# A second gate beside the attention steps: its calls spread anew over four steps, its softmax by tanh, another order within a step

## The chip, the core and the metric

The kernel runs on one core of one Trainium2 chip. The core has five engines with queues of their own: TensorE (PE in the profile; PEld is its weight load), VectorE (DVE), ScalarE (ACT), GpSimd (POOL) and SyncE (SP), which here only issues DMAs. The metric is the device time of one execution in microseconds.

## The reference

The input is x of 2 x 4096 tokens with 256 features. Three sublayers follow each other: half of a feed-forward network of experts, an attention of the delta-rule kind, and the same feed-forward network again with the same weights. All of it is in fp32.

```
x = x + 0.5 * ffn(layernorm(x))
x = x + attn(layernorm(x))
x = x + 0.5 * ffn(layernorm(x))

ffn:  scores = softmax(x @ gate_w)                  # 8 experts
      top_scores, top_idx = top_k(scores, 2)
      y = sum over the two of  (silu(xs@w1) * (xs@w3)) @ w2,   xs = score * x

attn: q, k, v = silu(causal conv of 4 taps (x @ Wq, Wk, Wv)),  4 heads of 64;  q, k normed
      beta = sigmoid(x @ Wb)
      chunks of 64 tokens, in order:  A = I + tril(Kb K^T, -1);  T = A^-1;  W = T Kb;  U = T Vb
      mid = U - W S^T;  O = Q S^T + (Q K^T * M) mid;  S += mid^T K
      out = rmsnorm(O) * rms_w @ Wo
```

## The kernel before, in words

Three programs follow each other: `ffn` (the first), `attention`, `ffn` (the second). A feed-forward part works on rows sorted by expert. So before it, a gate scores each token, picks its two experts and scatters the token's row into the lists of both. The first gate runs at the start of the first `ffn`. The second gate works on the result of the attention, and it is woven into `attention`: it is what this change is about.

`attention` goes over 32 steps. A step takes 128 tokens of each of the two sequences. It is a software pipeline of five depths: `body(f, g, t, s, u, v)` is called once per step for each engine, with `f` for the projections, convolution and silu of the newest tokens, `g` for the small matrices between keys, `t` for their inversion by blocks, `s` for the state, the output and its projection, `u` for what the gate needs of one step's result (a turn of it, its logits, its mean and variance), and `v = (n, c)` for the gate of block n, which is 4 steps (8 tiles of 128 tokens). c counts the four steps over which the calls of one block are spread. It goes 1, 2, 3 and then 0, and the texts below call these the phases: a step of phase 1 is one in which c is 1, and so on. `LAST` is 7, the last block. Each engine runs its calls strictly in the order in which `body` has them, and waits on semaphores for the others. There is no scheduler: the order is written by hand.

What the gate does, before the change:
- phase 1: GpSimd `gate_pow` (1/std), VectorE `gate_norm` (four small instructions) between `first_out32` and `out_scale`, and at the end of the step `gate_first` (the largest logit, five instructions).
- phase 2: VectorE `gate_second` (six) and `gate_sums` (three) behind the convolution; ScalarE `gate_exps`, an Exp, between `silus(f, 1)` and `silus(f, 2)`.
- phase 3: VectorE `gate_scores`, `gate_row_ends`, `gate_ends`, `gate_places`; TensorE `positions` (three fp32 products) ahead of `out_project`.
- The rows of a block are loaded by SP (`load_rows`, one 256 KB load in a step) and scattered by GpSimd (`gate_scatter`, one indirect DMA for each of the 8 tiles): three tiles in phase 0, two in phase 1, three in phase 2.

What bounds a step is a loop through the engines: `x_turn` (TensorE) turns the normed tokens, ScalarE and VectorE split them in a high and a low part (`x_high`, `x_low`), TensorE projects (`qkv`), ScalarE copies out (`raw_out`), VectorE does the convolution (18 instructions of `conv`, L1665), ScalarE the silus, TensorE turns keys and values back (`turn_back`, L1307 and L1313), ScalarE takes squares (L2090) and `norm_in` prepares the next tokens. Beside that, TensorE carries the chain of `t` and `s`: L1403 (`second_products32`, needs VectorE's `first_out32`, L1733), L1547 (`out_turn`, needs `out_scale`, L1770), L1415 and L1417 (`first_products64`, needs ScalarE's `second_out32`, L2136), L1556 (`out_project`), L1429 (`second_products64`), and of the gate L1448 (`gate_turn`) and L1462 (`gate_products`). `keep_busy` and `fill` (L1247) are products of the identity whose result nobody reads.

The inverses of the small blocks go through DRAM: SP stores them when GpSimd has solved them (`collect_inverses`, L1202), and loads them in another layout when that has landed (`place_inverses`, L1209). TensorE turns them in the next step (`turn16`, L1346).

## Time and profile before

| | us |
|---|---|
| median of three executions | 1480.89 |
| lowest, highest | 1477.67, 1484.17 |
| the profiled execution, its own time | 1484.35 |
| its span in the profile | 1482.7 |
| the 32 attention steps, first `x_turn` to last | 385.0 to 1124.8 |
| PE, DVE, ACT, POOL busy, of the span | 88%, 73%, 60%, 61% |

The shares are means over three programs with different limits. Between 475 and 1125 us, where all depths of the pipeline are filled, a step repeats every 22.9 to 26.4 us, and PE is busy in nearly all of it. Steps are told apart by the start of L1261, the first product of `x_turn`. A wait stands in square brackets behind the instruction that waited: `[1.82 <-ACT ws L2084]` means that the engine sat idle for 1.82 us, and what came last was ACT's line 2084. PE rows have their count in hardware instructions, two for one fp32 product.

### The profile page before, as it was taken

The numbers are of one execution on the slowest core, as the hardware profiler recorded it, in microseconds if no ns is written. First come the engines' busy times: TensorE is split into PE (matmuls) and PEld (weight loads), VectorE is DVE, ScalarE is ACT, GpSimd is POOL, SyncE is SP. The second block draws the span as 40 slices with busy tenths as digits, with TensorE's granted clock in tenths as the row PEclk, the third lists the DMA queues.
The fourth block names the chain that finished last, engine by engine and source line by source line (L and its number), as shares of the span: only waits on it lengthen the run. The fifth ranks groups of instructions, "written<-read, shape, count | busy, mean of one in ns | idle before, by whom it ended". The sixth has DMA issues, their size and how long they took to land. (4 is left out here: it accounts for less than half of the span.)

```text
span 1482.7 us, 46829 instructions
## 1 busy us (share of the span) xinstructions
PE 1298.2 (88%) x16868; PEld 1182.7 (80%) x16868; DVE 1088.9 (73%) x2864; ACT 892.4 (60%) x1836; POOL 909.3 (61%) x1595
## 2 busy tenths in 40 slices
PE   6974998898479999999989999999999836997997
PEld 6873997898468888888878887878788636997996
DVE  6874773676467888899888988899888464772674
ACT  2213772674356777768676767777777424772673
POOL 4872675377346557477667676766757651773567
PEclk7556999899689999999999999999999767998999
DMA  7537974784011222222232222222222276875782
GB/s 228 170 115 190 318 265 163 277 276 141 22 19 42 43 58 54 58 67 70 60 73 67 67 69 61 72 69 68 74 59 61 72 223 204 271 246 204 250 285 87
DMA packets 218560, 193.39 MB, mean 130 GB/s; under 512 B 105172, under 2 KB 182234, under 8 KB 218336
## 3 DMA queue, kind: packets, MB, share of 16 engines
q1 hardware_dynamic: 185056, 114.06, 28.5%
q0 software_dynamic: 24576, 67.94, 12.5%
q10 hardware_dynamic: 8704, 8.39, 2.0%
q8 instruction: 142, 2.33, 0.7%
q14 instruction: 82, 0.67, 0.2%
HBM read 102.63 MB, written 94.01 MB: 133 GB/s over the span
## 5 line engine op out<-in xcount | busy, mean ns | idle before, releaser
L1665 DVE SCALAR_TENSOR_TENSOR raw_w<-attn_raw,taps,raw_w 128x256 f32<-128x256 f32 x576 | 241.6, 482 | 4.4 <-ACT raw_w L2068 4.2
L494 PE MATMUL ffn_both<-ws,ffn_xhi 128*128 x1152 | 205.4, 290 | 0.6 <-issue 0.2
L494 PEld LDWEIGHTS ffn_both<-ws,ffn_xhi 128*128 128x128 f32 x1152 | 165.6, 193 | 3.1 <-issue 2.9
L2346 POOL TENSOR_TENSOR attn_inv<-attn_inv,attn_term 64x14 f32<-64x14 f32 (+6 forms) x448 | 137.4, 307 | 35.1
L2343 POOL TENSOR_TENSOR attn_term<-attn_small,attn_inv 64x14 f32<-64x14 f32 (+6 forms) x448 | 124.4, 278 | 32.6
L1268 PE MATMUL attn_fr<-attn_xhi,wqkv 128*128 128x256 f32 x768 | 139.7, 291 | 4.1 <-ACT attn_bth L2075 2.3
L517 PE MATMUL ffn_yb<-ws,ffn_hhi 128*128 x576 | 119.0, 291 | 6.2 <-DVE ffn_hlo L706 6.2
L2385 POOL TENSOR_TENSOR attn_factors<-attn_squared,attn_powers 128x10 f32<-128x10 f32 x28 | 55.1, 1969 | 109.9 <-DVE attn_squared L1763 109.9
L494 PE MATMUL ffn_both<-ws,ffn_xlo 128*128 x576 | 116.4, 284 | 0.0
L1268 PEld LDWEIGHTS attn_fr<-attn_xhi,wqkv 128*128 128x128 f32 x768 | 110.1, 192 | 7.5 <-ACT attn_bth L2075 3.0
L483 PE MATMUL ffn_both<-ident,ffn_xb 128*128 128x128 f32 x576 | 79.7, 284 | 41.4 <-ACT ffn_xb L795 25.3
L701 DVE TENSOR_TENSOR ffn_hid<-ffn_both,ffn_sil 128x512 f32<-128x512 f32 x72 | 49.8, 692 | 89.5 <-ACT ffn_sil L807 89.5
L869 POOL DMA_INDIRECT second_rows<-ffn_more_rows,ffn_to x64 | 63.1, 985 | 82.3 <-DVE ffn_to L679 66.3
L2059 ACT ACTIVATE attn_raw<-attn_fr 128x512 f32<-128x512 f32 x96 | 56.9, 592 | 92.6 <-PE attn_fr L1268 91.9
L807 ACT ACTIVATE ffn_sil<-ffn_both 128x512 f32<-128x512 f32 x72 | 43.0, 598 | 99.5 <-PE ffn_both L494 99.5
L483 PEld LDWEIGHTS ffn_both<-ident,ffn_xb 128*128 128x128 f32 x576 | 68.2, 147 | 43.3 <-issue 38.1
L795 ACT ACTIVATE ffn_xb<-ffn_more_rows 128x256 f32<-128x256 f32 x112 | 58.0, 591 | 72.5 <-DMA ffn_more_rows<-first_rows 41.3
L696 DVE TENSOR_TENSOR ffn_xlo<-ffn_both,ffn_xhi 128x1024 fp32r<-128x1024 f32 x72 | 87.8, 1219 | 16.8 <-ACT ffn_xhi L802 16.8
L517 PEld LDWEIGHTS ffn_yb<-ws,ffn_hhi 128*128 128x128 f32 x576 | 93.8, 190 | 7.2 <-issue 7.2
L494 PEld LDWEIGHTS ffn_both<-ws,ffn_xlo 128*128 128x128 f32 x576 | 90.7, 193 | 0.0
L802 ACT ACTIVATE ffn_xhi<-ffn_both 128x1024 fp32r<-128x1024 f32 x72 | 73.9, 1026 | 25.4 <-PE ffn_both L483 25.4
L2068 ACT ACTIVATE raw_w<-attn_raw,taps 128x256 f32<-128x256 f32 x192 | 87.1, 502 | 2.2
(333 smaller groups left out, 3861.5 us busy)
## 6 DMA issues: line engine op xcount, KB each, us to landing
ffn_xb<-second_rows SPq DMA_DIRECT2D x48, 259.0 KB
ffn_more_rows<-second_rows SPq DMA_DIRECT2D x48, 259.0 KB
raw_w<-second_rows SPq DMA_DIRECT2D x40, 259.0 KB
ffn_more_rows<-first_rows SPq DMA_DIRECT2D x64, 131.0 KB
ffn_xb<-in_L_attn_x_dram SPq DMA_DIRECT2D x8, 1024.0 KB, 5.7
attn_xin<-x_after_first ACTq DMA_DIRECT2D x32, 256.0 KB, 2.8
attn_xres<-x_after_first SPq DMA_DIRECT2D x32, 256.0 KB, 3.5
x_after_attention<-attn_xres SPq DMA_DIRECT2D x32, 256.0 KB, 2.2
```

Of the source, the lines that this page charges most:

```text
L483: last = pe.transpose(tr[:, q, j * P:(j + 1) * P], xs[:, k % 2, j, q * P:(q + 1) * P], ident[:])
L494: last = pe.matmul(hp[:, j, :], (xhi, xlo)[b][:, k % 2, q, j * P:(j + 1) * P], ws[:, bass.ds(experts[j], 1), a, q].rearrange("p o d -> p ( ...
L517: last = pe.matmul(yb[:, j, :], (hhi, hlo)[b][:, k % 2, j * P:(j + 1) * P], ws[:, bass.ds(experts[j], 1), a, 2].rearrange("p o d -> p (o d)"),
L696: dve.tensor_tensor(xlo[:, k % 2], tr, xhi[:, k % 2].bitcast(F32), ALU.subtract).then_inc(xlo_ready, 1)
L795: last = act.activation(xs[:, k % 2, j], row[:, DM:2 * DM], ACT.Identity, scale=row[:, c:c + 1], bias=row[:, c + 1:c + 2])
L802: act.activation(xhi[:, k % 2], tr, ACT.Copy).then_inc(xhi_ready, 1)
L869: pool.indirect_dma_start(out=rows2 if k < NSP else sums, out_offset=bass.IndirectOffsetOnAxis(ap=to[:, k % NW, j:j + 1], axis=0), in_=xw[ ...
L1268: last = pe.matmul(out, w[:, a, q, col], (xhi, xlo)[b][:, q, :], skip_group_check=True, start=(start and k == 0 and q == 0), stop=(k == 2 ...
L1665: dve.scalar_tensor_tensor(acc[:, j, r], raw[:, j, r, :, tap:tap + P], taps[:, j, r, tap:tap + 1], acc[:, j, r], ALU.mult, ALU.add)\
L2068: act.activation(acc[:, j, r], raw[:, j, r, :, 0:P], ACT.Copy, scale=taps[:, j, r, 0:1])\
L2343: pool.tensor_tensor(term[:, 0:k, 0:j], n[:, j + 1:, j:j + 1].broadcast_to([BP, k, j]), v[:, j:j + 1, 0:j].broadcast_to([BP, k, j]), ALU.m ...
L2346: pool.tensor_tensor(v[:, j + 1:, 0:j], v[:, j + 1:, 0:j], term[:, 0:k, 0:j], ALU.subtract)\
```

## The change

- The calls of the gate's block are spread otherwise: `gate_sums` goes from phase 2 to phase 3, `gate_scores`, `gate_row_ends` and `gate_places` from phase 3 to phase 0; `gate_norm` stands ahead of `first_out16` instead of behind `first_out32`; the scatters are three in phase 1, two in phase 2, three in phase 3. Blocks 6 and 7 keep the old spread in the main.
- The softmax of the gate uses e^x = (1 + tanh(x/2)) / (1 - tanh(x/2)): ScalarE takes a Tanh (which `beta_tanh`, L2075, uses in each step anyway) behind `second_out64`, and VectorE three more instructions on 128x72 values.
- Within a step the order of calls is another on TensorE (`gate_turn`, `gate_products`, `positions` and `state_in` stand later), on VectorE (`gate_products_out` is last), on ScalarE (`gate_turned` behind `out_turned`) and on SP (the result is stored behind `collect_inverses`, rows are loaded behind the residual).

```diff
@@ SP
-            def load_rows(v, c):
-                n = v[0]
+            def load_rows(v):
+                n, c = v
+                if c == 1 and 0 < n < LAST:
+                    load_step(n - 1, 3)
+                if n < LAST - 1 and c != 1:
+                    load_step(n, (c - 2) % 4)
+                if (n, c) in ((LAST - 1, 2), (LAST, 3)):
+                    for i in range(4):
+                        load_step(n, i)
...
                 if s:
                     load_residual(s)
                     if s[0] == NS - 1:
                         load_weights()
+                if v:
+                    load_rows(v)
+                if g:
+                    collect_inverses(g)
+                if s:
                     store_result(s)
                 if g:
-                    collect_inverses(g)
                     place_inverses(g)
@@ TensorE
+            def early_positions(v, u):
+                positions(v, u)
+
             def body(f, g, t, s, u, v):
-                if v and v[1] == 3 and v[0] == LAST - 1:
-                    positions(v, u)
...
                 if s:
-                    state_in(s, v)
+                    out_in(s)
                 if f:
                     x_turn(f)
                 if s:
-                    out_in(s)
+                    state_in(s, v)
+                if v and v[1] == 3 and (v[0] == LAST - 1):
+                    early_positions(v, u)
...
-                if u:
-                    gate_turn(u)
                 if t:
                     second_products32(t)
...
                 if u:
-                    gate_products(u, v)
+                    gate_turn(u)
                 if t:
                     first_products64(t)
-                if v and v[1] == 3 and v[0] != LAST - 1:
-                    positions(v, u)
                 if s:
                     out_project(s)
                 if t:
                     second_products64(t)
+                if u:
+                    gate_products(u, v)
                 if f:
                     turn_back(f)
+                if v and v[1] == 3 and (v[0] != LAST - 1):
+                    positions(v, u)
@@ VectorE
                 dve.wait_ge(gexp_ready, n + 1)
+                dve.tensor_scalar(lexp[:], ltanh[:], -1.0, 1.0, ALU.mult, ALU.add).then_inc(gscl_part, 1)
...
+                dve.reciprocal(lexp[:], lexp[:]).then_inc(gscl_part, 1)
...
+                dve.scalar_tensor_tensor(lexp[:], ltanh[:], 1.0, lexp[:], ALU.add, ALU.mult).then_inc(gscl_part, 1)
...
+                if v and v[1] == 1:
+                    gate_norm(v)
                 if t:
                     first_out16(t)
...
-                if v and v[1] == 1:
-                    gate_norm(v)
                 if s:
                     out_scale(s)
                 if f:
                     conv(f, 1, 3)
                     conv(f, 2, 1, 2)
-                if v and v[1] == 3 and v[0] != LAST - 1:
-                    gate_scores(v)
-                    gate_row_ends(v)
+                    conv(f, 2, 3)
+                if v and v[1] == 2:
+                    gate_second(v)
                 if f:
                     betas(f)
-                    conv(f, 2, 3)
+                if v and v[1] == (3 if v[0] == LAST else 0) and (v[0] != LAST - 1):
+                    gate_scores(v)
...
-                if v and v[1] == 2:
+                if v and v[1] == (2 if v[0] >= LAST - 1 else 3):
                     gate_sums(v)
                 if u:
                     gate_stats(u)
+                if v and v[1] == 1:
+                    gate_first(v)
+                if v and v[1] == (3 if v[0] == LAST else 0) and (v[0] != LAST - 1):
+                    gate_row_ends(v)
+                if more:
+                    norm_shift(after(f))
                 if s:
                     residual(s)
...
+                if f:
+                    norms(f)
+                if v and v[1] == 3 and (v[0] != LAST - 1):
+                    gate_ends(v)
+                if v and v[1] == (3 if v[0] == LAST else 0) and (v[0] != LAST - 1):
+                    gate_places(v)
                 if u:
                     gate_products_out(u, v)
-                if f:
-                    norms(f)
@@ ScalarE
-                act.activation(lexp[:], lsub[:], ACT.Exp).then_inc(gexp_ready, 1)
+                act.activation(ltanh[:], lsub[:], ACT.Tanh, scale=0.5).then_inc(gexp_ready, 1)
...
-                if u:
-                    gate_turned(u)
                 if t:
                     second_out32(t)
                 if s:
                     out_turned(s)
+                if u:
+                    gate_turned(u)
...
-                if v and v[1] == 2:
-                    gate_exps(v)
                 if f:
                     silus(f, 2)
                 if t:
                     second_out64(t)
+                if v and v[1] == 2:
+                    gate_exps(v)
@@ GpSimd
                 if v and v[1] == 1:
                     gate_pow(v)
-                if v and v[1] == 1 and 0 < v[0] < LAST:
-                    gate_scatter((v[0] - 1, 1), 4, 5)
-                if v and v[1] == 2 and 0 < v[0] < LAST:
-                    gate_scatter((v[0] - 1, 2), 5, 6)
+                if v and v[1] == 1 and (0 < v[0] < LAST):
+                    gate_scatter((v[0] - 1, 0), 1, 2)
+                if v and v[1] == 2 and (0 < v[0] < LAST):
+                    gate_scatter((v[0] - 1, 1), 3, 4)
                 if s and more:
                     both_factors(s, f)
...
+                if v and v[1] == 2 and (0 < v[0] < LAST):
+                    gate_scatter((v[0] - 1, 1), 4, 5)
+                if v and v[1] == 1 and (0 < v[0] < LAST):
+                    gate_scatter((v[0] - 1, 0), 2, 3)
...
+                if v and v[1] == (2 if v[0] == LAST - 1 else 3) and (0 < v[0] < LAST):
+                    gate_scatter((v[0] - 1, 2), 7, 8)
                 if g:
                     invert_blocks(g, 1, SB // 2 - 2)
                     invert_blocks(g, SB // 2 - 2, SB - 1)
```

On TensorE, from `fill` to `turn_back`, the order before is this (attn_sc<-attn_xres is `gate_turn`, attn_sc<-attn_gws,attn_gT is `gate_products`):

```order
L1247 MATMUL attn_fr<-ident 128x128 x4
L1448 MATMUL attn_sc<-ident,attn_xres 128x128 x4
L1403 MATMUL attn_tp<-attn_x,attn_i 64x64 x8
L1547 MATMUL attn_ob<-ident,attn_on 128x128 x4
L1462 MATMUL attn_sc<-attn_gws,attn_gT 64x8 x8
L1415 MATMUL attn_tp<-ident,attn_tb 64x64
...
L1556 MATMUL attn_ob<-wos,attn_oT 128x256 x4
L1429 MATMUL attn_tp<-raw_w,attn_tt 64x64 x8
L1307 MATMUL attn_fr<-ident,ws 128x128 x8
```

And in the changed kernel, on the same engine in the same step:

```order
L1252 MATMUL attn_fr<-ident 128x128 x4
L1408 MATMUL attn_tp<-attn_x,attn_i 64x64 x8
L1552 MATMUL attn_ob<-ident,attn_on 128x128 x4
L1453 MATMUL attn_sc<-ident,attn_xres 128x128 x4
L1420 MATMUL attn_tp<-ident,attn_tb 64x64
...
L1561 MATMUL attn_ob<-wos,attn_oT 128x256 x4
L1434 MATMUL attn_tp<-raw_w,attn_tt 64x64 x8
L1467 MATMUL attn_sc<-attn_gws,attn_gT 64x8 x8
L1312 MATMUL attn_fr<-ident,ws 128x128 x8
```

`gate_turn` has moved behind `out_turn`, and `gate_products` from behind `out_turn` to just ahead of `turn_back`.

On VectorE, the end of a step of phase 0 before (attn_ss<-raw_w begins `norms`, attn_glg<-attn_sc is `gate_products_out`, the last three rows are `gram_out` of the next step):

```order
L1647 SCALAR_TENSOR_TENSOR attn_nmr<-attn_mv,attn_factors 128x2
L1787 BN_STATS attn_gstats<-attn_xres 128x6 x2
L1790 BN_AGGR attn_gmv<-attn_gstats 128x2 x2
L1780 TENSOR_TENSOR attn_xres<-attn_ob,attn_xres 128x512
L1798 COPY attn_glg<-attn_sc 128x16
L1682 TENSOR_REDUCE attn_ss<-raw_w 128x16
L1685 RECIPROCAL attn_rk<-attn_ss 128x8
L1689 TENSOR_TENSOR attn_cc<-attn_beta,attn_rk 128x32
L1698 TENSOR_TENSOR raw_w<-attn_tp,attn_cc 128x256
L1703 TENSOR_TENSOR raw_w<-attn_tp,attn_cc 64x256
L1705 TENSOR_TENSOR ws<-attn_tp,attn_upto 128x2x256
```

And in the changed kernel, on VectorE at the end of a step of phase 0 (attn_chosen begins `gate_places`):

```order
L1788 TENSOR_TENSOR attn_xres<-attn_ob,attn_xres 128x512
L1690 TENSOR_REDUCE attn_ss<-raw_w 128x16
L1693 RECIPROCAL attn_rk<-attn_ss 128x8
L1697 TENSOR_TENSOR attn_cc<-attn_beta,attn_rk 128x32
L1924 TENSOR_TENSOR attn_chosen<-attn_picked,attn_row 128x128
L1926 TENSOR_REDUCE attn_slot<-attn_chosen 128x16
L1930 CAST attn_slots<-attn_slot 128x8
L1931 COPY attn_xg<-attn_slot 128x8
L1806 COPY attn_glg<-attn_sc 128x16
L1706 TENSOR_TENSOR raw_w<-attn_tp,attn_cc 128x256
L1711 TENSOR_TENSOR raw_w<-attn_tp,attn_cc 64x256
L1713 TENSOR_TENSOR ws<-attn_tp,attn_upto 128x2x256
```

`gate_places` and the copy of the logits now stand between `norms` and the next step's `gram_out`.

On SP, one step's DMAs before (x_after_attention<-attn_xres is the store of a step's result, small_inverses is `collect_inverses`, attn_i<-small_inverses `place_inverses`):

```order
L1194 DMA attn_small<-small_blocks 64x16x16
L1172 DMA attn_xg<-x_after_attention 128x2x256
L1160 DMA attn_xres<-x_after_first 128x2x256
L1165 DMA x_after_attention<-attn_xres 128x2x256
L1202 DMA small_inverses<-attn_inv 64x256
L1209 DMA attn_i<-small_inverses 128x8x16
```

And in the changed kernel, on SP:

```order
L1204 DMA attn_small<-small_blocks 64x16x16
L1161 DMA attn_xres<-x_after_first 128x2x256
L1182 DMA attn_xg<-x_after_attention 128x2x256
L1212 DMA small_inverses<-attn_inv 64x256
L1166 DMA x_after_attention<-attn_xres 128x2x256
L1219 DMA attn_i<-small_inverses 128x8x16
```

The 256 KB store has moved between the two transfers of the inverses, and the residual is loaded ahead of the gate's rows.

## Rows read from the trace of the kernel before

**Rows 1.** Busy time in stretches: start:end, length, engines, TensorE clock, DMA share, GB/s.
```profile
567.30:1124.80 557.50, 530.72 (x9167) 459.76 (x9168) 494.39 (x1423) 412.07 (x939) 377.81 (x836) 0.99 0.27 66
685.96:712.16 26.20, 24.11 (x398) 21.02 (x398) 23.00 (x66) 19.92 (x44) 18.20 (x39) 0.93 0.28 70
735.79:760.16 24.37, 22.78 (x397) 19.63 (x397) 19.89 (x55) 17.36 (x41) 16.45 (x35) 1.00 0.33 83
835.34:858.30 22.96, 22.66 (x398) 19.66 (x398) 19.88 (x55) 17.13 (x41) 16.95 (x36) 1.00 0.33 88
858.30:882.13 23.83, 22.80 (x397) 19.63 (x398) 21.84 (x64) 17.27 (x41) 18.74 (x42) 1.00 0.28 68
882.13:906.96 24.83, 22.71 (x398) 19.63 (x398) 22.03 (x64) 19.85 (x44) 16.66 (x37) 1.00 0.27 67
906.96:930.86 23.90, 23.46 (x403) 20.32 (x403) 21.85 (x67) 17.23 (x41) 14.37 (x34) 1.00 0.23 54
```

**Rows 2.** Timeline of PE, one step without second-gate work: start, duration, what.
```profile
557.91 0.60 PE L1448 MATMUL attn_sc<-ident,attn_xres 128*128 128x128 f32 x4
558.44 0.46 PE L1403 MATMUL attn_tp<-attn_x,attn_i 64*64 64x64 f32 x16
558.84 0.65 PE L1547 MATMUL attn_ob<-ident,attn_on 128*128 128x128 f32 x4
...
563.15 1.09 PE L1307 MATMUL attn_fr<-ident,ws 128*128 128x128 f32 x8
```

**Rows 3.** Timeline of PE, step at 453.08, the only one without L1448 and L1462.
```profile
466.80 0.46 PE L1403 MATMUL attn_tp<-attn_x,attn_i 64*64 64x64 f32 x16
467.40 0.66 PE L1547 MATMUL attn_ob<-ident,attn_on 128*128 128x128 f32 x4
```

**Rows 4.** Timeline of DVE in the step of rows 2.
```profile
557.67 0.42 DVE L1733 TENSOR_TENSOR attn_x<-attn_tp,attn_own 128x256 f32<-128x256 f32 x1
558.01 0.68 DVE L1770 TENSOR_TENSOR attn_on<-attn_ob,attn_factors 128x512 f32<-128x512 f32 x1
...
565.34 1.22 DVE L1682 TENSOR_REDUCE attn_ss<-raw_w 128x16 f32<-128x1024 f32 x1 [1.57 <-ACT raw_w L2090]
```

**Rows 5.** Groups of instructions on ACT: line, count, busy us, mean ns.
```profile
L2183 ACT ACT_TABLE_LOAD x7 | 9.0, 1283 | 0.1
...
L2084 ACT ACT_TABLE_LOAD x6 | 7.7, 1283 | 0.1
```

**Rows 6.** Timeline of PE, a step of phase 2.
```profile
902.80 1.09 PE L1307 MATMUL attn_fr<-ident,ws 128*128 128x128 f32 x8 [1.82 <-ACT ws L2084]
```

**Rows 7.** Timeline of DVE and of PE, a step of phase 1.
```profile
867.25 0.42 DVE L1718 TENSOR_TENSOR attn_x<-attn_tp,attn_own 128x256 f32<-128x256 f32 x1 [1.20 <-PE attn_tp L1358]
...
873.66 0.66 PE L1547 MATMUL attn_ob<-ident,attn_on 128*128 128x128 f32 x4 [0.51 <-DVE attn_on L1770]
```

**Rows 8.** Timeline of DVE, a step of phase 3.
```profile
926.42 0.28 DVE L1910 TENSOR_TENSOR attn_chosen<-attn_picked,attn_row 128x128 f32<-128x128 f32 x1
...
927.16 0.16 DVE L1917 COPY attn_xg<-attn_slot 128x8 f32<-128x8 f32 x1
```

**Rows 9.** Timeline of the queue of SP, three places.
```profile
859.02 0.47 SPq L1202 DMA_DIRECT2D small_inverses<-attn_inv  x1
861.01 0.37 SPq L1209 DMA_DIRECT2D attn_i<-small_inverses  x1
...
689.48 0.36 SPq L1209 DMA_DIRECT2D attn_i<-small_inverses  x1
```

**Rows 10.** Timeline of PE, start of the step at 760.16.
```profile
767.18 0.30 PE L1346 MATMUL attn_tp<-ident,attn_i 128*128 128x128 f32 x1 [0.53 <-DMA attn_i<-small_inverses]
```

**Rows 11.** DMA issues between 835 and 931 us: count, KB each, us to landing.
```profile
x_after_attention<-attn_xres SPq DMA_DIRECT2D x4, 256.0 KB, 2.7
```

**Rows 12.** Timeline of DVE and of PE where the last step begins.
```profile
1187.60 0.69 DVE L1780 TENSOR_TENSOR attn_xres<-attn_ob,attn_xres 128x512 f32<-128x512 f32 x1 [3.88 <-DMA attn_xres<-x_after_first]
...
1188.51 1.17 PE L1493 MATMUL attn_sc<-attn_state,ws 128*128 128x128 f32 x4 [2.25 <-DVE attn_glg L1798]
```

More of the change, by code:

```diff
@@ L1946, in body @@
                     remainder(s)
-                if v and v[1] == 3 and v[0] == LAST - 1:
-                    gate_ends(v)
-                    gate_scores(v)
-                    gate_row_ends(v)
-                    gate_places(v)
+                if v and v[1] == 3 and (v[0] == LAST - 1):
+                    early_rows(v)
                 if g:
@@ L1979, in body @@
                     conv(f, 2, 1, 2)
-                if v and v[1] == 3 and v[0] != LAST - 1:
-                    gate_scores(v)
-                    gate_row_ends(v)
+                    conv(f, 2, 3)
+                if v and v[1] == 2:
+                    gate_second(v)
                 if f:
                     betas(f)
-                    conv(f, 2, 3)
+                if v and v[1] == (3 if v[0] == LAST else 0) and (v[0] != LAST - 1):
+                    gate_scores(v)
+                if f:
                     if isinstance(f[0], int) and f[0] == 0:
                         clear_buffers()
-                if t and isinstance(t[0], int) and (t[0] == 0):
-                    column_sums_out()
-                if v and v[1] == 3 and v[0] != LAST - 1:
-                    gate_ends(v)
-                if v and v[1] == 2:
-                    gate_second(v)
-                if more:
-                    norm_shift(after(f))
-                if v and v[1] == 3 and v[0] != LAST - 1:
-                    gate_places(v)
-                if v and v[1] == 2:
+                if v and v[1] == (2 if v[0] >= LAST - 1 else 3):
                     gate_sums(v)
@@ L2224, in body @@
                     first_out64(t)
-                if v and v[1] == 2:
-                    gate_exps(v)
                 if f:
```

47 lines of the change are left out of this document (22 added, 25 removed).

## The prediction, made before the changed kernel had run

> **What bounds the kernel now.** I read the stretches first, cut at the starts of L1261, because the change touches only the attention steps. 23 steps with gate work take 557.50 us, and their lengths differ by phase: 22.96 in phase 0, 23.83 in phase 1, 24.83 in phase 2, 23.90 in phase 3 [rows 1]. In phase 0, which has three scatters but no gate arithmetic, PE is busy 22.66 of 22.96 us. So the step without gate work is a TensorE step: what PE waits is what the step grows by. The reader is to see that in the waits of PE: 1.82 us ahead of `turn_back` in phase 2 [rows 6], 0.51 ahead of `out_turn` in phase 1 [rows 7]. Three of the six steps of phase 2 are longer still: 26.20 at a mean granted clock of 0.93 [rows 1], which is one stretch at 1.2 instead of 2.4 GHz right behind such a wait. Last, one of two late steps of phase 0 takes 24.37 instead of 22.96 [rows 1], with PE waiting for DVE, which waited for small blocks from DRAM.
>
> In the step of rows 2 PE runs without a gap from L1448 at 557.91 to L1307 at 563.15, 5.24 us. DVE has 1.57 us to spare ahead of `norms` [rows 4].
>
> **The change part by part.**
>
> *Table loads.* Exp costs a load of ScalarE's table before it and one after it, 1.283 us each [rows 5]; they stand ahead of the last silu. The Tanh needs none: each step has a Tanh and silus, and the profile has no load between them. PE's wait of 1.82 goes; DVE's work of phase 2 (22.03 busy against 19.88 in phase 0, [rows 1]) lay behind the convolution anyway. Phase 2 then costs what a step without gate work costs: -1.87 in each of 6 steps, and -1.37 more in the three with the low clock (26.20 - 24.83), since the wait that preceded it is gone: 15.3 us of the 557.50.
>
> The Trainium skill (ScalarE: Activation LUTs, What ACT_TABLE_LOAD costs) adds a drain of about 1380 ns to each switch, 2.66 us for one. By that page two switches would be 5.3 us and phase 2 would gain over twice as much. The trace does not agree: the step is 1.87 us longer, and two bare loads with the Exp are 2.8.
>
> *`gate_norm` earlier.* In phase 1 its 0.7 us now fall in DVE's wait ahead of `first_out16` (1.20 us, rows 7) instead of ahead of `out_scale`. PE's 0.51 goes, and with it the 0.87 by which phase 1 is longer, 6 times. If GpSimd's `gate_pow` came late, up to 0.5 of each would stay.
>
> *The order on TensorE.* This is the cost, and it is paid in every step. The same products stand between `fill` and `turn_back`, but `gate_turn` no longer covers the wait for `first_out32`. DVE ends L1733 at 557.67 + 0.42 = 558.09 [rows 4]; PE is free at 557.91 [rows 2], so L1403 starts at about 558.15: 0.24 idle. It takes 0.40; then `out_turn` needs L1770, done at 558.69: start 558.75, 0.20 idle. The step at 453.08 has no `gate_turn`, and there L1547 follows L1403 by 0.60 instead of 0.40, which is this second wait [rows 2, 3]. Everything behind follows without a gap, `gate_products` too, and `turn_back` starts 0.44 later. Bounds: 0 if DVE's chain came earlier by as much; 0.53, the whole slot of `gate_turn`, from above. I take 0.44. `gate_products_out` behind `norms` delays `gram_out`, for which `gram(g, 1)` waits: 0.08. Together 0.52: a step without gate work, and one of phase 1 or 2, takes 23.48.
>
> *Phase 3.* `positions` moves from one place on PE's full path to another (0.7 us, 23.46 against 22.7 busy), so its cost stays: 22.96 + 0.44 + 0.70 = 24.10. The late copy and `gate_ends`, behind `norms`, are covered there, since `positions` makes PE the later one.
>
> *Phase 0.* Behind the convolution come `gate_scores` with three more instructions, and `gate_row_ends`. DVE is busy 1.97 more in phase 3 than in phase 0 [rows 1], of which `gate_places` is 0.81 (926.42 to 927.16 and 0.16, less the overlap, [rows 8]); so scores, row ends and ends are 1.2 at most. The three new ones on 72 columns are not in the trace: between 0.16 each, as for 8 columns [rows 8], and 1.22, as for 1024 [rows 4]. I take 0.28 each, near the lower end, as 72 is near 8: 0.85. Cover: 1.57 + 0.44 + 0.16 (the copy left) = 2.17, against 2.05. It just holds; what they take more than 1.0 in sum is on the path, up to 2.7 in each of 5 steps at the upper end. `gate_places` (0.81) now stands between `norms` and `gram_out`, on the path to `gram(g, 1)` and `qkv`; about 0.15 of it is slack: +0.65, so 24.13 with what follows. Before, all of it lay in DVE's spare time of phase 3.
>
> *Scatters and loads.* Phase 0 loses its three scatters in a row, and with them steps as the one of 24.37 and the one behind it, which waited 0.53 for the inverses [rows 10]. But phase 1 gets a third scatter, phase 3 two in a row and a third. I put 2.5 for such late steps, about two as the one of 24.37 [rows 1]; the bounds are 0 and rival B.
>
> *The tail.* In the last but one step the residual's load was stuck behind the gate's rows on SP; DVE waited 3.88 for it, and PE 2.25 for the logits' copy behind it [rows 12]. Now the residual is loaded first. PE gains 2.3 to 2.7; the three more instructions in `early_rows` (0.8) and the eight scatters behind them give back a part: -1.9. The head of the program and both feed-forward parts have no term.
>
> Sum: of the 23 steps 12 are of phases 1 and 2 (12 x 23.48 = 281.8), 6 of phase 3 (144.6), 5 of phase 0 (120.7). That is 547.1, with 2.5 for late steps 549.6, against 557.50: -7.9. Four full steps ahead of them without gate work pay 0.52 each, +2.1. With the tail, -7.7. Against the profiled execution's own 1484.35 (span 1482.7 and 1.65 around it) that is 1476.7. It lies 3.5 above the median of 1480.89; from the median the forecast is 1473.2, and I say **1473**.
>
> **The rivals.** What a measurement here can tell from no change is 0.5%, 7.4 us: faster is below 1473.5, slower above 1488.3.
>
> *A: PE does not pay.* The two idle pieces on PE are absorbed, because `x_turn`'s loop has slack that the trace hides (silus done earlier, ACT's `out_turned` no longer behind `gate_turned`). For it: without `gate_turn` and `gate_products`, 1.1 us of PE work, L1547 of the step at 453.08 still waited for DVE [rows 3], so another chain is near. Against: in rows 2 PE has no gap. The time: 0.44 in 27 steps, 12 less: 1461.
>
> *B: the scatters hurt more.* The step that read its small blocks late paid 24.37 - 22.96 = 1.41 [rows 1]. DVE's L1733 is now just what PE waits for, so any lateness goes through. If 9 of the 12 steps of phases 1 and 3 pay it: 12.7 less the 2.5 given back, +10: 1484. For it: both had a scatter in flight. Against: phase 2 had scatters in the same places and was never late.
>
> *C: slower, the store between the inverses.* `collect_inverses` is issued at 859.02 and has landed at 861.01, when `place_inverses` goes out [rows 9]. The 256 KB store now goes at +0.47 and takes 2.7 to land [rows 11], 1.2 us after `place_inverses` was issued. If that one can only land behind it, `turn16` is late by 1.2 less its slack. The slack is at least 0.8: in the step that starts at 685.96 it went out 3.52 after the start, against 2.71 in the step at 858.30, and PE did not wait [rows 1, 9]. So 0.4 in 21 steps, and the full 1.2 in 6 of phase 1, where the slack can be none [rows 10]: +15.6, 1489. It decides from a delay of 0.8 on.
>
> The Trainium skill (DMA: Bandwidth & Descriptors, Queues, rings and completion order) speaks for C: descriptors of SP's queue are consumed in ring order on each DMA engine, and a semaphore's increment lands only after every earlier write of that engine. By that rule the inverses' landing waits for the store's. No row of before shows the two in flight together.
>
> That the change does not do what it says is out: the changed order on ScalarE has no table load in attention at all.
>
> **How the numbers follow.** Forecast 0.51 (its own range 1467 to 1480, so 0.28 faster and 0.23 the same), A 0.17, B 0.17, C 0.15. Faster 0.45, same 0.40, slower 0.15. The range for 8 in 10 reaches from A, a little below it, to just short of C: 1460 to 1488.
>
> **What would show it.** Phases 1 and 2 at 23.5, phase 3 and phase 0 with what follows it at 24.1; no load on ScalarE between the silus; the clock at its upper level throughout; PE waiting about 0.2 ahead of L1408 and of L1552 in each step; `gram_out` 0.8 later behind a phase 0. Steps without gate work at 22.9 would speak for A; DVE waiting for small blocks in phases 1 and 3 for B; PE waiting at `turn16` (now L1351) for C. The forecast is wrong if the steps without gate work stay as they were, or if PE waits more than 1 us anywhere in a step.

## The result, and the profile after

The changed kernel took 1475.15 us (median of 20 runs, 1471.45 to 1478.97) against 1478.73 for the kernel before (20 runs, 1470.94 to 1488.80) on the same chip: ratio 0.9966, 95% interval [0.9954, 0.9978], so 0.3% faster: a small gain that the interval shows, and no difference by the bound of 0.5% that the prediction set. Measured again later it was 0.9979 [0.996, 0.9997] where before took 1480.06, and 0.9927 [0.9901, 0.9952] on a chip where before took 1627.97. Why the change is worth more on that one turned out to be one of the findings.

The profiled execution took 1472.86 (span 1471.2), 2.3 below its median; that of before was 5.6 above its own. So 11.5 us lie between the two traces and 3.6 between the medians. The stretches are those of [rows 1], cut at L1266: 23 steps, then one without gate work and one each of phase 1, 2, 3 and 0 (start:end, length, busy PE, PEld, DVE, ACT, POOL, clock, DMA share, GB/s).

```profile
565.17:1109.77 544.60, 527.10 (x9168) 456.96 (x9168) 495.94 (x1428) 395.13 (x927) 376.72 (x837) 1.00 0.27 67
541.86:565.17 23.31, 22.79 (x397) 19.67 (x398) 19.86 (x55) 17.13 (x41) 13.87 (x35) 1.00 0.20 48
849.36:873.48 24.12, 22.85 (x397) 19.67 (x397) 22.28 (x68) 17.13 (x41) 19.26 (x40) 1.00 0.29 74
873.48:896.83 23.35, 22.84 (x398) 19.70 (x398) 21.38 (x61) 17.30 (x42) 16.07 (x37) 1.00 0.28 70
896.83:920.84 24.01, 23.18 (x403) 20.41 (x404) 21.08 (x60) 17.20 (x41) 17.61 (x40) 1.00 0.29 74
920.84:944.09 23.25, 22.74 (x399) 19.62 (x398) 21.70 (x63) 17.05 (x40) 13.62 (x33) 1.00 0.24 60
```

The reader is to see three things. PE's busy time of a step hardly moved (22.79 against 22.66), yet the step without gate work is 0.38 longer than the same step before (23.31 against 22.93): PE idles in it. Phase 2 is no longer a long step, and the clock is 1.00 in all 23 steps. Phase 1 is now the longest; the phase 3 shown here is one that waited 0.40 for its small blocks.

The idle of PE in a step without gate work is where the prediction put it. L1408 starts at 13.80 behind the step's start and `gate_turn` started at 13.54 before, so 0.26; L1552 follows L1408 by 0.60 instead of 0.40 [rows 2]. Timeline of PE, the changed kernel:

```profile
555.66 0.46 PE L1408 MATMUL attn_tp<-attn_x,attn_i 64*64 64x64 f32 x16
556.26 0.66 PE L1552 MATMUL attn_ob<-ident,attn_on 128*128 128x128 f32 x4
556.76 0.60 PE L1453 MATMUL attn_sc<-ident,attn_xres 128*128 128x128 f32 x4
```

In a phase 1 that has a `gate_places` behind the norms of the step before it, PE waits for `gram_out`, and in the last step but one of the attention for the inverses (timeline of PE and of SP's queue, the changed kernel):

```profile
851.60 0.43 PE L1335 MATMUL attn_tp<-ws 64*64 64x128 f32 x7 [0.69 <-DVE ws L1713]
...
1155.52 0.58 SPq L1166 DMA_DIRECT2D x_after_attention<-attn_xres  x1
1157.02 0.36 SPq L1219 DMA_DIRECT2D attn_i<-small_inverses  x1
...
1160.17 0.30 PE L1351 MATMUL attn_tp<-ident,attn_i 128*128 128x128 f32 x1 [3.30 <-DMA attn_i<-small_inverses]
```

At the end of the attention, where the pipeline runs empty, a long wait of PE is new: 5.41 ahead of the last `out_turn`. GpSimd had two scatters ahead of `attn_factors` (L2394), which `out_scale` (L1778) needs, although VectorE had made what L2394 needs (`attn_squared`) by 1180.82. Timeline of GpSimd, VectorE and TensorE, the changed kernel:

```profile
1180.31 1.01 POOL L2300 DMA_INDIRECT first_rows<-attn_xg,attn_slots  x1 [3.04 <-DVE attn_xg L1931]
1180.65 0.17 DVE L1771 SCALAR_TENSOR_TENSOR attn_squared<-attn_ss,attn_oms 128x8 f32<-128x8 f32 x1
1181.62 0.96 POOL L2300 DMA_INDIRECT first_rows<-attn_xg,attn_slots  x1 [0.30 <-issue]
1182.61 1.67 POOL L2394 TENSOR_TENSOR attn_factors<-attn_squared,attn_powers 128x8 f32<-128x8 f32 x1
1184.31 0.69 DVE L1778 TENSOR_TENSOR attn_on<-attn_ob,attn_factors 128x512 f32<-128x512 f32 x1 [2.38 <-POOL attn_factors L2394]
1185.06 1.11 PE L1552 MATMUL attn_ob<-ident,attn_on 128*128 128x128 f32 x4 [5.41 <-DVE attn_on L1778]
```

And at the same place in the kernel before, where GpSimd starts L2375 as soon as `attn_squared` is there:

```profile
1195.57 1.67 POOL L2375 TENSOR_TENSOR attn_factors<-attn_squared,attn_powers 128x8 f32<-128x8 f32 x1 [0.81 <-DVE attn_squared L1763]
1196.74 0.63 PE L1448 MATMUL attn_sc<-ident,attn_xres 128*128 128x128 f32 x4 [2.35 <-DVE attn_state L1753]
1198.02 0.66 PE L1547 MATMUL attn_ob<-ident,attn_on 128*128 128x128 f32 x4 [0.65 <-DVE attn_on L1770]
```

The three instructions that the softmax gained, and the reduction beside them (timeline of DVE, a phase 0):

```profile
1032.74 0.20 DVE L1884 TENSOR_SCALAR attn_lexp<-attn_ltanh 128x72 f32<-128x72 f32 x1
1032.98 0.60 DVE L1886 RECIPROCAL attn_lexp<-attn_lexp 128x72 f32<-128x72 f32 x1
1033.62 0.23 DVE L1888 SCALAR_TENSOR_TENSOR attn_lexp<-attn_ltanh,attn_lexp 128x72 f32<-128x72 f32 x1
1033.88 0.22 DVE L1890 TENSOR_REDUCE attn_lsum<-attn_lexp 128x8 f32<-128x64 f32 x1
```

### The profile page after: what moved, and what is told of

Read it like the earlier page. It is cut to its first block and busy times, and to the rows that moved or that the text cites. A ratio compares the mean times of both kernels' runs of the same rounds, so it can differ in the third digit from the quotient of the medians.

```text
span 1471.2 us, 46839 instructions
## 1 busy us (share of the span) xinstructions
PE 1285.3 (87%) x16868; PEld 1170.2 (80%) x16868; DVE 1094.8 (74%) x2888; ACT 873.2 (59%) x1822; POOL 905.6 (62%) x1595
```

## The experiments

Twelve kernels ran, in three groups of four. Groups 1 and 2 ran on chips where the kernel before took 1616.7 and 1628.0 us (medians), group 3 on one where it took 1480.1. The table has the median length of a step by phase, over the steps 11 to 30 (counted from 0, with starts read to 0.01), the sum of the 27 steps that the prediction priced, from the traces, and the measured ratio to the kernel before. Compare within a group. Each row of step lengths is one execution. Group 1 has only variants: the changed kernel itself did not run in it.

| kernel | no gate work | phase 1 | 2 | 3 | 0 | 27 steps | ratio |
|---|---|---|---|---|---|---|---|
| before, first trace | 22.94 | 23.84 | 26.19 | 23.63 | 22.96 | 649.3 | |
| changed, first trace | 23.32 | 24.12 | 23.35 | 23.69 | 23.27 | 637.9 | 0.9966 |
| group 1: e1_store | 23.35 | 24.45 | 23.45 | 24.59 | 23.26 | 643.3 | 0.9920 |
| e2_turn | 23.40 | 24.46 | 23.39 | 24.57 | 23.35 | 644.2 | 0.9910 |
| e3_places | 23.34 | 24.29 | 23.47 | 24.55 | 23.25 | 642.6 | 0.9907 |
| e4_tanh | 22.94 | 24.32 | 23.35 | 25.32 | 25.88 | 662.6 | 0.9995 |
| group 2: b0_before | 22.94 | 24.61 | 24.82 | 23.68 | 25.43 | 660.0 | |
| a0_after | 23.34 | 24.45 | 23.47 | 24.66 | 23.25 | 644.0 | 0.9927 |
| e5_exp | 23.34 | 24.46 | 24.02 | 24.51 | 23.27 | 646.4 | 0.9937 |
| e7_order | 23.12 | 24.22 | 23.04 | 24.57 | 22.98 | 640.3 | 0.9865 |
| group 3: a1_after | 23.33 | 24.06 | 23.33 | 23.68 | 23.26 | 636.8 | 0.9979 |
| f0_spread | 23.34 | 24.18 | 23.35 | 23.66 | 23.28 | 636.4 | 0.9975 |
| f1_order_spread | 22.95 | 23.84 | 22.94 | 23.66 | 22.98 | 632.1 | 0.9935 |
| f2_exp_late | 22.94 | 24.17 | 24.04 | 24.20 | 22.96 | 646.9 | 0.9998 |

**e1_store: does the store between the inverses cost anything?** (rival C)

```diff
-                if g:
-                    collect_inverses(g)
                 if s:
                     store_result(s)
                 if g:
+                    collect_inverses(g)
                     place_inverses(g)
```

> The changed kernel, but SP stores a step's result ahead of collect_inverses again, as before the change. My theory: in the full steps nothing moves (23.3, 24.1, 23.7 us by phase, as in the changed kernel), because place_inverses lands before TensorE gets to turn16; in the last but one step turn16 waits less (3.30 us in the changed kernel, here about 2.5), and the whole is 0 to 1 us faster than the changed kernel. Rival (the store between the two transfers costs in every step): steps become 0.3 to 0.4 us shorter, the whole 10 us faster than the changed kernel.

1603.13 us, ratio 0.992 [0.989, 0.995]. In the steps nothing moved: turn16 goes out 6.4 behind the start in both orders, and the table's line is that of the other kernels of the group. In the last step but one PE waits 1.94 for the inverses instead of 3.13 in `e2_turn`, and gives it back right behind, where it waits 1.26 for VectorE. So C's mechanism shows in one step at most. That it is worth nothing in the end is argued from this, since the unaltered kernel did not run in this group: the steps show no cost, and the ratios of the three variants lie within each other's intervals. The rule of the Trainium skill that spoke for C (DMA: Bandwidth & Descriptors, Queues, rings and completion order) agrees with that one step at most: `attn_i` landed 3.15 after its issue there in the changed kernel, and 2.37 in `e1_store`, where the store goes first.

**e2_turn and e7_order: what the order on TensorE costs, and why.** The first puts `gate_turn` alone back ahead of `second_products32`:

```diff
+                if u:
+                    gate_turn(u)
                 if t:
                     second_products32(t)
                 if s:
                     out_turn(s)
-                if u:
-                    gate_turn(u)
                 if t:
                     first_products64(t)
```

> The changed kernel, but gate_turn stands ahead of second_products32 on TensorE again. My theory (the two idle pieces of TensorE, ahead of second_products32 and out_turn, are the 0.38 us by which each step without gate arithmetic grew): a step takes 22.95 instead of 23.33, turn_back starts 18.8 after x_turn instead of 19.2, phases 2 and 0 gain 0.38 too, the whole about 10 us faster than the changed kernel. Rival (gate_products just ahead of turn_back is what made it late): steps stay at 23.3, the whole is the same within 2 us.

1603.46, ratio 0.991 [0.9879, 0.9942]: no step became shorter. The waits ahead of L1408 and L1552 went, and one ahead of `first_products64` came, for ScalarE's copy of what L1408 made (timeline of PE, this kernel):

```profile
573.43 0.60 PE L1453 MATMUL attn_sc<-ident,attn_xres 128*128 128x128 f32 x4
573.96 0.46 PE L1408 MATMUL attn_tp<-attn_x,attn_i 64*64 64x64 f32 x16
574.35 0.66 PE L1552 MATMUL attn_ob<-ident,attn_on 128*128 128x128 f32 x4
575.38 0.24 PE L1420 MATMUL attn_tp<-ident,attn_tb 64*64 64x64 f32 x1 [0.37 <-ACT attn_tb L2155]
```

So my reading of the mechanism was short by a link. Three trips away from TensorE and back stand in a row here, and as I read it both gate calls are needed to fill them. The second kernel restores both, and ScalarE's order with them (`gate_turned` ahead of `second_out32`). The two were not separated; but the earlier place of `gate_turned` can only hold up the copy L2155 for which PE waited, not bring it forward:

```diff
@@ TensorE
+                if u:
+                    gate_turn(u)
                 if t:
                     second_products32(t)
...
                 if u:
-                    gate_turn(u)
+                    gate_products(u, v)
                 if t:
                     first_products64(t)
...
-                if u:
-                    gate_products(u, v)
@@ ScalarE
+                if u:
+                    gate_turned(u)
                 if t:
                     second_out32(t)
                 if s:
                     out_turned(s)
-                if u:
-                    gate_turned(u)
```

> The changed kernel with gate_turn ahead of second_products32 and gate_products ahead of first_products64 on TensorE, gate_turned ahead of second_out32 on ScalarE, as in the kernel before; all else as changed. Theory (three round trips stand in a row there, second_products32, out_turn, first_products64, and both gate calls are needed to fill their waits): steps without gate work 22.93 instead of 23.3, phase 2 22.95, phase 3 23.3; phase 0 stays at 23.2, where VectorE is as late as TensorE; phase 1 0.2 to 0.4 shorter. 8 to 10 us faster than the changed kernel. Rival (the late gate_products is what makes the squares or the logits' copy fit, and the step has another bound at 23.3): steps stay at 23.3 and the time within 2 us.

1608.70, ratio 0.9865 [0.9837, 0.9894], 7.4 us less than the changed kernel in its group. Undisturbed steps are 22.94 to 22.98, 0.4 shorter, phase 2 0.43, phase 0 0.27 (I had expected it to stay). Phase 3 stays at 24.57, where I had expected 23.3; it is 24.66 in `a0_after`. Two of the four steps without gate work are longer, one of them because VectorE waited 1.39 for the small blocks. PE from `gate_turn` on, without a gap:

```profile
627.81 0.60 PE L1453 MATMUL attn_sc<-ident,attn_xres 128*128 128x128 f32 x4
628.34 0.46 PE L1408 MATMUL attn_tp<-attn_x,attn_i 64*64 64x64 f32 x16
628.73 0.65 PE L1552 MATMUL attn_ob<-ident,attn_on 128*128 128x128 f32 x4
629.32 0.64 PE L1467 MATMUL attn_sc<-attn_gws,attn_gT 128*64 128x8 f32 x16
629.89 0.27 PE L1420 MATMUL attn_tp<-ident,attn_tb 64*64 64x64 f32 x1
```

**e3_places: `gate_places` off the path.** In blocks 0 to 5 it runs ahead of `first_out16` instead of behind the norms.

```diff
+                if v and v[1] == 0 and v[0] < LAST - 1:
+                    gate_places(v)
                 if t:
                     first_out16(t)
...
-                if v and v[1] == (3 if v[0] == LAST else 0) and (v[0] != LAST - 1):
+                if v and v[1] == 3 and v[0] == LAST:
                     gate_places(v)
```

> The changed kernel, but gate_places of blocks 0 to 5 stands in phase 0 ahead of first_out16, where VectorE waits 0.88 us for TensorE, instead of behind norms. My theory (gate_places behind norms holds up gram_out and with it gram(g, 1) and qkv of the step of phase 1): x_turn to turn16 (6.4 us elsewhere) falls from 7.17 to 6.4 in phase 1, steps of phase 1 take 23.4 instead of 24.1, the whole 4 to 5 us faster. Rival (phase 1 is long for its own work, gate_norm ahead of first_out16 or its scatters): phase 1 stays at 24.1, the whole is the same.

1601.92, ratio 0.9907 [0.9876, 0.9937]. turn16 of phase 1 goes out at 6.46 instead of 7.17, so the 0.7 is what `gate_places` costs there. But the step is only 0.16 shorter: VectorE's L1726 then waits 1.0 to 1.1, until 0.4 to 0.5 after the end of the scatter beside it, though TensorE's L1363, for which it waits, had ended 0.9 to 1.0 earlier. That `gate_places` delays turn16 by 0.7 is shown. That the scatter took most of the gain is argued; on a chip of the other kind the kernel did not run.

**e4_tanh, e5_exp and f2_exp_late: what the softmax by tanh is worth.** The first is the kernel before with only the softmax changed; the second the changed kernel with only the softmax changed back; the third the kernel before with one call moved.

```diff
@@ e4_tanh, ScalarE and VectorE; e5_exp has it the other way round
-                act.activation(lexp[:], lsub[:], ACT.Exp).then_inc(gexp_ready, 1)
+                act.activation(ltanh[:], lsub[:], ACT.Tanh, scale=0.5).then_inc(gexp_ready, 1)
@@ f2_exp_late, ScalarE, in the kernel before
-                if v and v[1] == 2:
-                    gate_exps(v)
                 if f:
                     silus(f, 2)
                 if t:
                     second_out64(t)
+                if v and v[1] == 2:
+                    gate_exps(v)
```

> The kernel before, with only the softmax by tanh: no table loads, three more VectorE instructions in gate_scores in phase 3, ahead of the last convolution taps. My theory: phase 2 falls from 24.83 (26.2 with the low clock) to 22.95 and no step of it has the low clock; phase 3 grows from 23.6 to 24.6 to 24.9, as the three instructions (1.24 us in the changed kernel's trace) are on the path there. Together 15.3 less and 7 more: 8 us faster than before. Rival (the loads are hidden, and the order made phase 2 shorter): phase 2 stays at 24.8, the whole is 5 us slower than before.

> The changed kernel with Exp in place of Tanh, and so without the three added VectorE instructions; Exp at the place that the change gave to the Tanh, behind second_out64. Theory: two table loads of 1.28 come back ahead of the squares in phase 2, PE waits about 1.8 ahead of turn_back, the steps of phase 2 are 1.8 longer (25.1) and some fall to a low clock behind it; phase 0 is at most 0.1 shorter, since the three instructions lay in VectorE's spare time: 11 to 15 us slower than the changed kernel. Rival (the gain is the spreading, not the tanh: the longer phase 2 gives GpSimd room, and what comes behind it gets shorter): within 4 us of the changed kernel.

> The kernel before with one call moved: gate_exps, still an Exp, behind second_out64 instead of between the two silus. Theory (what costs is that the table loads stand ahead of the last silu; behind second_out64 ScalarE waits for turn_back anyway): phase 2 23.4 to 23.6 instead of 24.8, turn_back at 18.8 instead of 20.7; GpSimd's third scatter of phase 2 then stands in the next step and takes 1.5 of phase 3, so the time is 0 to 3 us shorter than before, as with tanh alone. Rival (loads cost wherever they stand): phase 2 stays at 24.8.

`e4_tanh` took 1616.50, ratio 0.9995 [0.9977, 1.0013]: phase 2 fell to 23.35 (I had said 22.95), and the time stayed, where I had said 8 us faster. Phase 3 is 25.32 against 23.68 in `b0_before`, for two reasons. The three new instructions take 1.2 there, ahead of the last taps of the convolution, so ScalarE's silu L2091 waits 2.78 for them instead of 1.54. And GpSimd still has a scatter of phase 2 to issue when the step starts; L1719 is 0.5 later than in `b0_before`. Timeline of VectorE and ScalarE in `e4_tanh`:

```profile
876.16 0.43 DVE L1719 TENSOR_TENSOR attn_x<-attn_tp,attn_own 128x256 f32<-128x256 f32 x1 [0.90 <-PE attn_tp L1359]
...
884.16 0.28 DVE L1877 TENSOR_SCALAR attn_lexp<-attn_ltanh 128x72 f32<-128x72 f32 x1
...
887.38 0.63 ACT L2091 ACTIVATE ws<-raw_w 128x512 f32<-128x512 f32 x1 [2.78 <-DVE raw_w L1666]
```

`e5_exp` took 1617.99, ratio 0.9937 [0.9914, 0.9959], only 1.9 us more than the changed kernel, and the two intervals overlap: phase 2 is 0.55 longer, not 1.8. `f2_exp_late` took 1478.93, ratio 0.9998 [0.9977, 1.0019]; turn_back is back at 18.78 and the step at 24.04, above the 23.4 to 23.6 that I had said. Its phase 3, with no new instruction but with the scatter of phase 2 at its start, is 24.20 against 23.63 before, 0.6 longer and not 1.5. All three say the same of the loads: the place decides. Timeline of ScalarE in `e5_exp`:

```profile
968.82 0.65 ACT L2158 ACTIVATE attn_tb<-attn_tp 64x256 f32<-64x256 f32 x2 [0.39 <-PE attn_tp L1434]
969.49 1.28 ACT L2196 ACT_TABLE_LOAD   x1
970.78 0.26 ACT L2196 ACTIVATE attn_lexp<-attn_lsub 128x72 f32<-128x72 f32 x1
970.95 1.00 ACT L2103 ACTIVATE raw_w<-attn_fr 128x1024 f32<-128x1024 f32 x1
```

Here one load stands ahead of the squares and not two: the squares need none of their own, nor does the Tanh of the next step, and the second load comes ahead of that step's first silu, where it lengthens nothing that is seen (phase 3 24.51 against 24.66). My expectation of 1.8 had both on the path. The load takes 1.28 and the next instruction starts 0.01 behind it, so the drain that the Trainium skill adds (ScalarE: Activation LUTs, What ACT_TABLE_LOAD costs) is not seen here either.

**b0_before, a0_after, a1_after: the same two kernels on the other chips.**

> The kernel before, unaltered, for a trace beside the others of this group. Theory (tanh alone brings GpSimd's scatters into the steps behind it): steps of phase 3 at 23.6 to 23.9 and of phase 0 at 23.0 here too, against 25.2 to 25.7 and 25.8 to 26.0 in the kernel with tanh alone. Rival (it is the chip on which that one ran): phases 3 and 0 are 25 to 26 us here as well.

> The changed kernel itself, unaltered, for its trace beside the other kernels of this group. Theory (its own parts give the gain, on any chip): ratio to the kernel before 0.990 to 0.997, steps without gate work 23.3 to 23.4, phase 2 23.4. Rival (the ratios near 0.991 of the three variants with one edit undone came from those edits): this one at 0.997 and they at 0.991, so 6 to 9 us slower than each of them.

> The changed kernel again, unaltered, for its trace and its ratio beside the others of this group. Theory (the gain over the kernel before depends on whether ScalarE and VectorE are held while scatters follow each other): if the steps of phase 3 are 24.6 here, the ratio is 0.990 to 0.994 as in the last group; if they are 23.7 to 24.0, it is 0.995 to 0.998 as in the first measurement. Rival (the ratio has nothing to do with it): any other pairing.

`b0_before`: 1630.50 in one run. a0: 1616.11, ratio 0.9927 [0.9901, 0.9952]; a1: 1477.59, ratio 0.9979 [0.996, 0.9997]. Both pairings came as expected. My theory of phase 0 in `e4_tanh` fell: `b0_before` has 25.43 there as well, so phase 0 is long on such a chip without the tanh. Phase 3, at 23.68 in `b0_before`, is long by the tanh's doing. What the chips differ in is seen where three scatters follow each other. In `b0_before` ScalarE is held for 2.56 us, until 0.73 after the last of them, though what it needs was made in time:

```profile
914.38 1.15 PE L1515 MATMUL attn_sc<-ws,raw_w 128*64 128x64 f32 x32
...
914.71 0.96 POOL L2281 DMA_INDIRECT first_rows<-attn_xg,attn_slots  x1 [0.30 <-issue]
...
915.98 0.96 POOL L2281 DMA_INDIRECT first_rows<-attn_xg,attn_slots  x1 [0.30 <-issue]
917.67 0.66 ACT L2159 ACTIVATE attn_mid<-attn_sc 128x256 f32<-128x256 f32 x2 [2.56 <-remote]
```

In `f2_exp_late`, on the chip of group 3, the same instructions stand as close, and ScalarE does not wait:

```profile
929.04 0.96 POOL L2281 DMA_INDIRECT first_rows<-attn_xg,attn_slots  x1 [0.30 <-issue]
929.94 0.85 ACT L2159 ACTIVATE attn_mid<-attn_sc 128x256 f32<-128x256 f32 x2
930.31 0.99 POOL L2281 DMA_INDIRECT first_rows<-attn_xg,attn_slots  x1 [0.30 <-issue]
```

**f0_spread and f1_order_spread: a better version.** The first spreads the scatters of blocks 0 to 4 evenly, two in each of the four phases, never in a row; the second has the order of `e7_order` too.

```diff
@@ GpSimd, ahead of inverse_std
+                if v and 0 < v[0] < LAST - 1 and v[1] != 1:
+                    gate_scatter((v[0] - 1, 2), 2 * ((v[1] - 1) % 4), 2 * ((v[1] - 1) % 4) + 1)
@@ GpSimd, behind both_factors
+                if v and 0 < v[0] < LAST - 1:
+                    gate_scatter((v[0] - 1, 1), 2 * ((v[1] - 1) % 4) + 1, 2 * ((v[1] - 1) % 4) + 2)
@@ the other gate_scatter calls of a block, now for block LAST - 1 alone
-                if v and v[1] == 1 and (0 < v[0] < LAST):
+                if v and v[1] == 1 and v[0] == LAST - 1:
                     gate_scatter((v[0] - 1, 0), 1, 2)
```

> The changed kernel with the scatters of blocks 0 to 4 spread evenly: two in each of the four phases, one early (behind remainder_scaled) and one late (behind both_factors), never two in a row. Theory (a chip where ACT's mid_out waits until the scatters in a row have ended pays for pairs): phase 3 at 23.7 instead of 24.6, phase 1 at 24.1 instead of 24.4, phases 2 and 0 at 23.5 and 23.3; 6 to 8 us faster than the changed kernel where that one has 24.6 in phase 3, and within 2 us of it on a chip like the first. Rival (what costs is the number of scatters, not that they stand in a row): phase 0, which gets two, becomes 0.5 longer or more and the time stays.

> Both together: the gate's calls on TensorE and ScalarE at their old places, and the scatters spread evenly. Theory: the two do not touch each other, steps without gate work 22.94, phase 2 23.1, phase 0 23.0, phase 1 23.8, phase 3 23.4; 13 to 16 us faster than the changed kernel, ratio to the kernel before 0.982 to 0.985 on a chip like the last two. Rival (with TensorE no longer late, the small blocks from DRAM and GpSimd are): 8 us faster, as with the order alone.

f0: 1475.56, ratio 0.9975 [0.9959, 0.9991], 2 us less than the changed kernel, as said for such a chip; phase 0 stayed at 23.28 with two scatters in it, so their number costs nothing on this chip. Whether it brings 6 to 8 us on a chip of the other kind was not tried. f1: 1469.59, ratio 0.9935 [0.9912, 0.9957], 8.0 less than the changed kernel and the fastest here. I had said 13 to 16. The steps are as expected (22.95, 22.94, 22.98) except phase 3 at 23.66; of the 10.4 that 27 steps shorter by 0.385 would have given, 4.7 stand in the 27 steps of the trace, since three of them (24.56, 25.07, 24.47) read the small blocks late: VectorE's L1721 waited 5.8 for them in the 27 steps, against 1.8 in `a1_after`. That is the rival's point.

## Why the prediction was right

The forecast of 1473 was 2.2 below the measured median. The mechanism of the steps was right in the main, but the closeness of the time owes something to luck: the change was forecast at -7.7 and the medians moved by -3.6, and the forecast started from a median of 1480.89 that turned out 2.2 above that of 20 runs. In the trace the 27 steps gained 5.6 more than was said and the tail 5.2 less, and these two errors cancel. No rival came about in its size; B's mechanism did in part. Step by step:

- *Table loads.* Phase 2 takes 23.35 instead of 23.48, in all six steps, at a clock of 1.00. The size was right, the reason half of it. I gave it all to the Tanh; the changed kernel with Exp loses only 2.4 of 644.0 in the 27 steps, because the change also moves the call. And in the kernel before neither edit alone brought anything that can be measured: the shorter phase 2 leaves GpSimd's third scatter to phase 3, and with the Tanh phase 3 has the three instructions on its path as well. So it takes the new spreading, of the scatters and of `gate_scores`, for the gain to count; that is argued, as no run has the one without the other. The prediction put the low clock down to PE's wait of 1.82. In the kernel before, a stretch at 1.2 GHz follows three of the six such waits, and the changed kernel has neither in its 27 steps. But `f2_exp_late` has no PE wait over 1.2 in its steps and still two such stretches (steps of phase 1 of 26.41 and 26.78, clock 0.94), so the wait is not their only cause.
- *The order on TensorE.* Predicted 0.44 and 0.08 a step. Measured 0.38 in all; the 0.08 for the late copy did not show. The two idle pieces were where I put them, but the explanation missed the third trip (`e2_turn`): with `gate_turn` alone moved back the cost stays. Restoring both takes 0.4 off (`e7_order`). Rival A is out.
- *`gate_norm` earlier.* Right: the phase 1 that has no `gate_places` ahead of it, at 565.17, takes 23.33. The others pay 0.78 in turn16 (0.65 predicted), and some the late small blocks: 24.85 once, where L1721 waited 0.82.
- *Phase 3.* Predicted 24.10, measured 23.69 where the small blocks are on time. `positions` behind `turn_back` partly falls where PE waits for the next normed tokens anyway: it costs 0.35, not 0.70. Of the terms of a step this one was mis-sized most, 2.5 over six steps.
- *Phase 0.* The three added instructions take 1.14 from the start of the first to the start of the reduction, not 0.85, as the reciprocal of 72 columns takes 0.60. The cover just held: the norms start 21.31 behind the step's start, against 21.34 in a step without gate work. So 23.27.
- *Late DMA steps.* 2.5 was allowed for. Five steps of the changed trace stand above their phase's median, by 0.3, 0.7, 0.7, 0.3 and 0.2, which is 2.3 in sum. All five are of phases 1 and 3, and in each VectorE's L1721 waited for the small blocks (0.30 to 0.82). So the sign that was named for B is there, at 0.2 to 0.7 a step and not at 1.41 in nine of them. At B's size it is out on this chip. (B's sum gives 1483, not the 1484 that stands there.)
- *The tail.* Predicted -1.9; the stretch from the last `x_turn` to TensorE's first product in the second feed-forward part is 3.3 longer, 108.85 against 105.56. This is the term of the sum that was mis-sized most, by 5.2. In group 3 it is 111.26 in `a1_after` against 104.12 in `f2_exp_late`, which has the order of before there. The wait of 2.25 in rows 12 went as said, and others came: 3.30 for the inverses, 1.00 at L1498 for the logits' copy, and 5.41 ahead of `out_turn` in the last step, where before 2.35 and 0.65 stood ahead of `gate_turn` and `out_turn`. I had let the three instructions in `early_rows` and the scatters behind them give back 0.4 to 0.8 in all; two of the scatters hold `attn_factors` up by 1.8, for which VectorE and then PE wait. How much of the tail each wait is worth stays open: `e1_store` took 1.2 off the first without a gain that can be seen, and in `f1_order_spread` the tail is 105.57 with 2.36 ahead of `out_turn`.

The sum over 27 steps was 643.5 (549.6 and four of 23.48); the trace has 637.9. Against the other trace the steps gained 11.4 and not 5.8, the tail lost 3.3, and 3.4 more were gained in the head and the second feed-forward part, for which there was no term: together the 11.5 between the two traces. The medians moved by only 3.6. Before's profiled execution was a long one: its phases 2 of 26.2 with the clock at 0.93 do not come in each execution (`b0_before` has one of six). So a sum against that one execution misleads, and I had corrected for 3.5 of its 5.6 us only. What else an execution of 1471 and one of 1489 of the same kernel differ in stays open.

## What to carry to other kernels

A call of another chain that stands between two products may be what fills a wait, and a wait that it fills does not show in the trace before: before moving it, add up all trips away from the engine up to the next free work, not the first one. A table load costs by its place: between two silus of the path both loads were paid, and the step was 1.87 us longer; behind the path's last copy one was paid in part, 0.55 to 1.11, and the other not. And if a step gets shorter, ask which slower engine had used its length; here the fix of phase 2 paid nothing by itself, and did so only in the kernel that also moved the scatters and `gate_scores`. Last, look at the end of a pipeline by itself: there a call that was free in the full steps can stand alone ahead of what everybody waits for, as two scatters did here.

## What the runs showed of the hardware

Chips differ in how GpSimd's indirect DMAs stand beside the other engines. On the two with 1617 and 1628 us a waiting ScalarE or VectorE instruction started only 0.4 to 0.8 after the scatter or the last of a row had ended (0.14 once in `b0_before`); on the chips where before took 1480 it started at once. The feed-forward parts, full of such DMAs, show it as well: the same line in the kernel before, first on the chip of group 2, then in the first trace (line, count, busy, mean ns, idle before and what ended it).

```profile
L807 ACT ACTIVATE ffn_sil<-ffn_both 128x512 f32<-128x512 f32 x72 | 42.9, 595 | 148.6 <-remote 85.5
```

```profile
L807 ACT ACTIVATE ffn_sil<-ffn_both 128x512 f32<-128x512 f32 x72 | 43.0, 598 | 99.5 <-PE ffn_both L494 99.5
```

That this is one cause for both is argued, not shown; no run took the scatters away. It makes a scatter's place worth testing on more than one chip: the same change was worth 0.2 to 0.3% on one kind and 0.7% on the other. Exp, Square and Tanh ran from one table in `e5_exp` and `f2_exp_late`: the only loads are ahead of the Exp and ahead of the next silu. VectorE's RECIPROCAL takes 0.20 us on 128x8 and 0.60 on 128x72, where the instruction beside it takes 0.20 on the same 72 columns.
